# A convolution stage whose scores share TensorE's row strips with the maxima: strips 0 and 1 beside strips 2 and 3

## The reference, cut to what matters

```python
x = x + _L1_conv_ref(_gn(x), ...)

def _L1_conv_ref(x, wq, bq, wk, bk, wv, bv, fc1_w, fc1_b, fc2_w, fc2_b, fuse_w, fuse_b):
    q = conv2d(x, wq, bq, 'SAME').reshape(b, -1, hw)      # 16 channels, 3x3
    k = conv2d(x, wk, bk, 'SAME').reshape(b, -1, hw)      # 16 channels
    v = conv2d(x, wv, bv, 'SAME').reshape(b, c, hw)       # 64 channels
    attn = jnp.einsum('bci,bcj->bij', q, k) * scale
    attn = jax.nn.softmax(attn, axis=-1)
    local = jnp.einsum('bcj,bij->bci', v, attn).reshape(b, c, h, w)
    y = jnp.mean(x, axis=(2, 3))
    y = jax.nn.relu(y @ fc1_w.T + fc1_b)
    y = jax.nn.sigmoid(y @ fc2_w.T + fc2_b)
    glob = x * y[:, :, None, None]
    cat = jnp.concatenate([local, glob], axis=1)
    return conv2d(cat, fuse_w, fuse_b, 'VALID')           # 1x1
```

## Time and profile before

| what | value |
|---|---|
| device time, 3 runs | 11482.52, 11489.68, 11515.75 us; median 11489.68 |
| the profiled execution: its own time, its span | 11510.12 us, 11508.3 us |
| granted TensorE clock, mean of the span | 0.807 of full speed |
| busy in the span | PE 60%, DVE 64%, ACT 42%, POOL 63% |
| convolution stage: first operation of VectorE to its last write of the result | 6044.26 to 6660.72 us |
| products for the maxima (L809), in the stage | 256 MATMUL, 110.7 us busy, 47.9 us of idle TensorE before them |
| products of input and gated term (L867, L869) | 128 and 128 MATMUL |

### The profile page before, as it was taken

The page is one execution under the profiler, slowest core; times in us unless marked ns, Lnnn a source line. Parts: engine busy times, 40 slices in busy tenths (PEclk is TensorE's granted clock), DMA queues, the critical chain, the costliest instruction groups (busy, mean ns, idle before and its releaser), DMA issues. The chain is left out here.

```text
span 11508.3 us, 84579 instructions
## 1 busy us (share of the span) xinstructions
PE 6869.3 (60%) x21895; PEld 2896.9 (25%) x21895; DVE 7327.9 (64%) x5584; ACT 4837.5 (42%) x5351; POOL 7215.9 (63%) x4635
## 2 busy tenths in 40 slices
PE   0178888888888888888878979950000010000569
PEld 0133333333333333333333323320000000000432
DVE  8689999999999999999992257741111111112334
ACT  0066666666666666666652236631111111110123
POOL 0078888888888888888873220017777777775037
PEclk8599999999999999999997679975555555555569
DMA  0145555555555555555551000012222222220022
GB/s 9 31 134 155 152 157 154 156 156 154 156 153 156 153 156 154 157 155 154 156 147 24 1 10 1 1 5 37 18 18 18 18 20 18 18 18 8 3 53 89
DMA packets 388258, 959.55 MB, mean 83 GB/s; under 512 B 124306, under 2 KB 159762, under 8 KB 385762
## 3 DMA queue, kind: packets, MB, share of 16 engines
q1 hardware_dynamic: 303106, 930.59, 29.2%
q0 software_dynamic: 75808, 26.27, 5.2%
q10 hardware_dynamic: 9216, 1.05, 0.1%
HBM read 905.24 MB, written 50.92 MB: 83 GB/s over the span
## 5 line engine op out<-in xcount | busy, mean ns | idle before, releaser
L502 POOL TENSOR_TENSOR hC<-h,Cb 128x1024 f32<-128x1024 f32 x1536 | 3610.4, 2359 | 936.5 <-DVE h L581 935.0
L581 DVE TENSOR_TENSOR_SCAN h<-dA,B_ps 128x1024 f32<-128x1024 f32 x1536 | 3512.4, 2287 | 68.1
L285 PE MATMUL y_ps<-hC,con 128*128 128x512 f32 x6144 | 2909.8, 595 | 92.5 <-DVE gz L587 56.9
L432 ACT ACTIVATE dA<-delta,negA 128x1024 f32<-128x1024 f32 x1536 | 1762.5, 1148 | 1835.6 <-DVE h L581 1835.0
L2514 POOL DMA_INDIRECT g_got<-scratch_node,g_idx x2048 | 1946.1, 950 | 614.4 <-issue 614.2
L573 DVE TENSOR_TENSOR B_ps<-dx,B_ps 128x1024 f32<-128x1024 f32 x1536 | 1856.3, 1208 | 93.2 <-PE B_ps L279 93.2
L2530 PE MATMUL g_ps_y<-g_wout,g_hid 128*128 128x64 f32 x512 | 126.2, 428 | 2248.4 <-ACT g_hid L2570 2248.4
L285 PEld LDWEIGHTS y_ps<-hC,con 128*128 128x128 f32 x6144 | 1136.9, 189 | 1127.3 <-issue 740.5
L279 PE MATMUL B_ps<-Bpart,sel 96*128 96x512 bf16 x3072 | 925.7, 383 | 676.0 <-DVE h L581 674.9
L2600 DVE TENSOR_TENSOR g_e<-g_tgt,g_got 128x128 f32<-128x128 f32 x64 | 27.1, 423 | 1759.9 <-DMA g_got<-scratch_node,g_idx 1759.9
L2554 ACT ACTIVATE g_w_ps<-g_w 128x128 f32<-128x128 f32 x64 | 18.0, 281 | 1941.2 <-DVE g_r L2615 1941.2
(11 more groups left out here) (470 smaller groups left out, 10158.7 us busy)
## 6 DMA issues: line engine op xcount, KB each, us to landing
Cb<-scratch_c_rows SPq DMA_DIRECT2D x3072, 256.0 KB, 3.9
g_got<-scratch_node,g_idx POOLq DMA_INDIRECT x2048
eb_share<-scratch_gate_rows SPq DMA_DIRECT2D x128, 256.0 KB, 3.4
scratch_edge<-g_out SPq DMA_DIRECT2D x64, 384.0 KB
par<-in_ssm SPq DMA_DIRECT2D x48, 395.5 KB, 5.0
scratch_c_rows<-Crow SPq DMA_DIRECT2D x96, 128.0 KB, 3.7
scratch_place<-s_zero SPq DMA_DIRECT2D x4, 1024.0 KB, 10.4
g_tgt<-scratch_place SPq DMA_DIRECT2D x1, 4096.0 KB, 20.8
```

Of the source, the lines that this page charges most:

```text
L285: last = nc.tensor.matmul(y_ps[:, hs], con[:, K_ID:K_ID + P], hC[k % DEEP][:, hs], start=(k == 0), stop=(k == STEPS - 1))
L432: A(dA[k % DEEP][:, :], delta[d][:, :], ACT.Exp, scale=negA[:, n:n + 1]).then_inc(decay_ready, 1)
L502: G.tensor_tensor(hC[k % DEEP][:, :], hst[k % DEEP][:, :], Cb[k % DEEP][:, :], ALU.mult).then_inc(prod_ready, 1)
L581: V.tensor_tensor_scan(hst[k % DEEP][:, ::step], dA[k % DEEP][:, ::step], B_ps[k % 2][:, ::step], 0.0, ALU.mult, ALU.add).then_inc(scanned, 1)
```

## The change

1. The maxima move to row strips 2 and 3 (partitions 64 to 127) and are issued one block to every slot, each half of them straight behind one half of the scores: strips 0, 2, 1, 3. They write other PSUM banks than the scores. A block's products start when `top_read` says that the block before was reduced; the image's first block also waits for `doubled`.
2. For that the queries and keys must lie on partitions 64 to 127 as well. VectorE copies them there (`double`): four copies of 64x512 after each of the first two groups of taps of a pair, 32 in all, each four behind a wait for `conv_read`.
3. Input and gated term of a pair are computed for both images at once with block-diagonal weights, as 128x128 products, in two halves ("res0", "res1", at u = 9 and 11 of the pair before), and go with the bias straight to `t_sb`. The image's fused output is added to `t_sb` later. The per-image event "res" in slot 3 is gone, and so is its place at the stage's end.
4. `search.first_level` is issued by VectorE after the first pair's preparation instead of ahead of it.

The diff, without constants, names and the packing of the weights:

```diff
@@ -655,23 +655,23 @@
 
     def maxima_at(g):
 
-        img, s = g // PER + 1, g % PER
-        return [(img, 2 * (s - 2) + k) for k in range(2)] if 2 <= s <= 5 and 0 <= img < B else []
+        img, i = divmod(g + PER + 2, PER)
+        return (img, i) if 0 <= img < B else None
 
     def events_at(g):
 
         out = []
         img, s = g // PER, g % PER
-        if s in (1, 2, 3) and 0 <= img - 1 < B:
-            out.append((("den", "out", "res")[s - 1], img - 1))
+        if s in (1, 2) and 0 <= img - 1 < B:
+            out.append((("den", "out")[s - 1], img - 1))
         if s == 6 and 0 <= img + 1 < B:
             out.append(("rows", img + 1))
         q, u = at_pair(g, 2)
         if q is not None and u in (8, 12, 13, 14):
             out.append(({8: "gm", 12: "gv", 13: "fc1", 14: "fc2"}[u], q))
         q, u = at_pair(g, 1)
-        if q is not None and u in (7, 15):
-            out.append((f"vt{u // 8}", q))
+        if q is not None and u in (7, 9, 11, 15):
+            out.append(({7: "vt0", 9: "res0", 11: "res1", 15: "vt1"}[u], q))
         return out
 
     def taps_at(g):
...
@@ -699,11 +699,11 @@
         cw = sb("cw", [P, CW_COLS])
         con = sb("con_c", [P, K_COLS])
         xc, sq = sb("cxc", [P, L]), sb("csq", [P, L])
-        xg = [sb(f"cxg{k}", [P, L]) for k in range(3)]
+        xg = [sb(f"cxg{k}", [P, L]) for k in range(2)]
         xpad = sb("xpad", [P, PW, PW])
         st = sb("st", [P, 16])
         S1, GM, S2, GV, YS, HID, Y, BQ = (st[:, i:i + 1] for i in range(8))
-        key, query = ([sb(f"c_{n}{k}", [2 * 32, L]) for k in range(4)] for n in ("key", "query"))
+        key, query = ([sb(f"c_{n}{k}", [P, L]) for k in range(4)] for n in ("key", "query"))
         v_sb = sb("v_sb", [P, L])
         vT = [sb(f"vT{k}", [P, PER, 2, C]) for k in range(2)]
         mrow = sb("mrow", [P, PER])
...
@@ -775,17 +775,29 @@
                 def dve(name, q):
                     pe.wait_ge(dve_done, dve_s.after(name, q))
 
-                def scores(g):
+                def scores(g, half):
 
                     img, j = divmod(g, PER)
-                    if j == 0:
+                    if j == 0 and half == 0:
                         pe.wait_ge(rows_in, img * 32 + 32)
-                    for half in range(2):
-                        if g:
-                            pe.wait_ge(exped, 2 * (g - 1) + half + 1)
-                        rows = strip(half)
-                        M(part_ps[half][:, :], key[img % 4][rows, j * P:(j + 1) * P], query[img % 4][rows, halves[half]],
-                          start=True, stop=True).then_inc(scored, 1)
+                    if g:
+                        pe.wait_ge(exped, 2 * (g - 1) + half + 1)
+                    rows = strip(half)
+                    M(part_ps[half][:, :], key[img % 4][rows, j * P:(j + 1) * P], query[img % 4][rows, halves[half]],
+                      start=True, stop=True).then_inc(scored, 1)
+
+                def maxima(img, i, half):
+                    n = maxima_no[img, i]
+                    if half == 0:
+                        if i == 0:
+                            pe.wait_ge(doubled, 2 * (img // 2) + 2)
+                        if n:
+                            pe.wait_ge(top_read, n)
+                    rows = strip(2 + half)
+                    last = M(top_ps[:, halves[half]], query[img % 4][rows, i * P:(i + 1) * P], key[img % 4][rows, halves[half]],
+                             start=True, stop=True)
+                    if half:
+                        last.then_inc(topped, 1)
 
                 def sums(g):
                     img, j = divmod(g, PER)
@@ -798,17 +810,6 @@
                         last = M(sum_ps[half * C:(half + 1) * C, :], vT[img // 2 % 2][:, j, img % 2, :], E[g % 4][:, halves[half]],
                                  start=j == 0, stop=j == PER - 1)
                     last.then_inc(summed, 1)
-
-                def maxima(img, i):
-                    n = maxima_no[img, i]
-                    if i == 0:
-                        pe.wait_ge(conv_read, 4 * (img // 2) + 2)
-                    if n:
-                        pe.wait_ge(top_read, n)
-                    for half in range(2):
-                        last = M(top_ps[:, halves[half]], query[img % 4][strip(half), i * P:(i + 1) * P],
-                                 key[img % 4][strip(half), halves[half]], start=True, stop=True)
-                    last.then_inc(topped, 1)
 
                 def taps(q, group, tap):
 
...
@@ -860,26 +861,25 @@
                             last = M(side_ps[:, k * P:(k + 1) * P], oT[at % 2][:, k * P:(k + 1) * P], cw[:, CW_FL:CW_FL + P],
                                      start=True, stop=True)
                     else:
-                        q, b = divmod(at, 2)
-                        dve("xg", q)
-                        rows = slice(b * C, (b + 1) * C)
-                        for i in BLK:
-                            M(side_ps[:, i * C:(i + 1) * C], x_sb[rows, q, i * P:(i + 1) * P], con[rows, K_ID + b * C:K_ID + (b + 1) * C],
-                              start=True, stop=False)
-                            last = M(side_ps[:, i * C:(i + 1) * C], xg[q % 3][rows, i * P:(i + 1) * P], cw[rows, CW_FG:CW_FG + C],
+                        dve("xg", at)
+                        for k in range(4):
+                            i = 4 * int(kind[-1]) + k
+                            M(side_ps[:, k * P:(k + 1) * P], x_sb[:, at, i * P:(i + 1) * P], con[:, K_ID:K_ID + P], start=True, stop=False)
+                            last = M(side_ps[:, k * P:(k + 1) * P], xg[at % 2][:, i * P:(i + 1) * P], cw[:, CW_FG:CW_FG + P],
                                      start=False, stop=True)
                     last.then_inc(side_made, 1)
 
                 pe.wait_ge(loaded, 32)
                 for g in slots:
-                    if 0 <= g < ALL:
-                        scores(g)
+                    for half in range(2):
+                        if 0 <= g < ALL:
+                            scores(g, half)
+                        if maxima_at(g):
+                            maxima(*maxima_at(g), half)
                     if 0 <= g - 1 < ALL:
                         sums(g - 1)
                     for event in events_at(g):
                         side(*event)
-                    for block_ in maxima_at(g):
-                        maxima(*block_)
                     for tap in taps_at(g):
                         taps(*tap)
 
@@ -989,6 +989,14 @@
                     if i == 0 and img:
                         dve.wait_ge(side_made, event_no["rows", img - 1] + 1)
                     V.reduce_max(mrow[:, i:i + 1], top_ps[:, :], AX).then_inc(top_read, 1)
+
+                def double(q, group):
+
+                    dve.wait_ge(conv_read, 4 * q + group + 1)
+                    for b in range(2):
+                        for t in (query, key):
+                            last = V.tensor_copy(t[(2 * q + b) % 4][C:P, halves[group]], t[(2 * q + b) % 4][0:C, halves[group]])
+                    last.then_inc(doubled, 1)
 
                 def side(kind, at):
 
@@ -1022,23 +1030,30 @@
                                         side_ps[:, :].rearrange("p (k h c) -> p h k c", k=4, h=2),
                                         rden[:, :].rearrange("p (h k) -> p h k", h=2).unsqueeze(3).broadcast_to([P, 2, 4, C]),
                                         ALU.mult).then_inc(side_read, 1)
+                        dve.wait_ge(side_read, event_no[kind, at] + 1)
+                        here = t_sb[:, at * PER:(at + 1) * PER, :]
+                        V.tensor_tensor(here, here, tmp[:, :, :], ALU.add).then_inc(fin, 1)
+                        dve.wait_ge(fin, at + 1)
                     else:
-                        V.tensor_tensor(tmp[:, :, :], tmp[:, :, :], side_ps[:, :].rearrange("p (i c) -> p i c", i=PER),
-                                        ALU.add).then_inc(side_read, 1)
-                        dve.wait_ge(side_read, event_no[kind, at] + 1)
-                        V.tensor_tensor(t_sb[:, at * PER:(at + 1) * PER, :], tmp[:, :, :],
-                                        cw[:, CR_FB:CR_FB + C].unsqueeze(1).broadcast_to([P, PER, C]), ALU.add).then_inc(fin, 1)
-                        dve.wait_ge(fin, at + 1)
+                        first = 2 * at * PER
+                        here = t_sb[:, first:first + 2 * PER, :].rearrange("p (b i) c -> p i b c", b=2)
+                        bias = cw[:, CR_FB:CR_FB + C].unsqueeze(1).unsqueeze(1).broadcast_to([P, 4, 2, C])
+                        V.tensor_tensor(here[:, 4 * int(kind[-1]):4 * int(kind[-1]) + 4, :, :],
+                                        side_ps[:, :].rearrange("p (i b c) -> p i b c", i=4, b=2), bias, ALU.add).then_inc(side_read, 1)
 
                 dve.wait_ge(loaded, 32)
                 dve.wait_ge(zeroed, 1)
                 V.tensor_scalar(BQ, cw[:, CV_BQ:CV_BQ + 1], SCALE, None, ALU.mult).then_inc(dve_done, 1)
```

(18 more changed lines are left out.)

2 lines of the change are left out of this document (1 added, 1 removed).

## The result

The change takes 11362.6 us (median of 4 runs, 11359.4 to 11374.62) against 11490.43 before (4 runs), a ratio of 0.988 [0.9869, 0.9892]: 128 us faster, where 90 were forecast. The profiled execution has its own time of 11365.2 us, a span of 11363.4 and a mean granted clock of 0.818.

What follows compares the result with a forecast made beforehand. TensorE was taken as the bound, often at 1.2 GHz. Tap halves -55, tap-free halves -13, last slots -11, end -8, start -4.5 sum to -91.5, called 90: 11420 profiled, 11400 median; range 11335 to 11445.

Steps and rivals of the forecast that it cites:

- the rival with the high clock: Four strips hold TensorE at 2.4 GHz in tap-free halves, last slots and start: gain 150 us, 11340; chance 17%.
- signs of being wrong: Tap halves above 70 us or clock below 0.7; fast tap-free halves; first score after 6135; late gathers; other stretches changing.
- Four strips run together: In the stage's slots, two score and two maxima products take one pair plus 0.07 us, 64 times: 4.5 us lost.
- the strips do not overlap: Score and maxima products wait at different times, each slot costs a pair more, some 85 us: 11485; chance 5%.
- The low clock in the tap-free halves and the last slots: TensorE stays mostly at 1.2 GHz there; tap-free halves gain only 13 us, the last 16 slots 11.
- Tap halves: The three halves with taps take 57.6, 62.4 and 62.4 us against 73.7, 82.9 and 80.9: 55 us gained.
- Four buffers of `E` cover: GpSimd's gathers end 12 us later; four buffers cover this until slot 4, else it costs a few us once.
- Copies of 0.4: Each of VectorE's 512-column copies in `double` takes 0.4 us; at 0.69 the gain is 7 us less.
- Start and end: Moving the search brings first scores 4.5 us earlier; one addition replacing "res" and its answers saves 8 us.
- slower: low clock through tap halves: Stalls in slots 2 and 4 keep tap halves at 1.2 GHz: 138 us more, a loss of 48, 11535; chance 3%.

Runs made afterwards that it cites:

- Experiment 1: The changed kernel with the maxima on strips 0 and 1 again, the copies still made but not read: 11466.18 us, ratio 0.9958 to the kernel before.
- part 3 alone: The kernel before with only the block-diagonal input and gated-term products for both images and the later addition of the fused output: 11460.39 us, ratio 0.9954.
- experiment 5: The changed kernel with VectorE reducing a slot's maxima before it answers the slot's event: 11293.39 us, ratio 0.981 to the kernel before.
- experiment 6: The changed kernel with VectorE's copies of queries and keys issued two slots later: 11348.44 us, ratio 0.9856 to the kernel before.
- experiment 3: The changed kernel with input and gated term computed per image by 64-row products in "res", as before: 11403.85 us, ratio 0.991 to the kernel before.
- experiment 7: The changed kernel with VectorE reducing before answering events and copies two slots later, run twice: 11281.98 and 11285.01 us, ratios 0.98 and 0.9802 to before.
- experiment 10: The changed kernel with reduction before answers, copies two slots later, and the search again ahead of the first reduction: 11302.66 us, ratio 0.9818 to before.
- experiment 9: The changed kernel with reduction before answers, copies two slots later, and GpSimd's gathers spread, 16 ahead then two per tap slot: 11278.37 us, ratio 0.9803.
- Experiment 4: The kernel before with only the search moved behind the first pair's preparation on VectorE, 10 runs: 11498.44 us, ratio 0.9989 to the kernel before.

## Why the prediction was right, and where it was off

The direction and the mechanism held, and 11362.6 lies in the range of 11335 to 11445. The size was off by 38 us. The gain of 128 lies outside the 65 to 120 that I called my forecast (57%) and short of the 150 of the rival with the high clock (17%); the range held it because it was drawn out to that rival. Of the signs of being wrong one came: tap-free halves near 43 us with a clock above 0.8, in two of three (44.74 and 38.95 us at 0.89 and 0.87).

- **Four strips run together**: right, but not 64 times. 1.07 us for four products against 1.05 + 0.07 forecast, in 20 slots; in 34 three halves run together behind the wait; ten blocks have no scores beside them. Experiment 1 puts the overlap, with the clock that goes with it, at 90 us of the 128. The rival "the strips do not overlap" would have been about even; with the same strips the kernel is at 11466.
- **The low clock in the tap-free halves and the last slots**: the step that failed. The prediction says "From here I take the low clock, as now", and wrote 56.9, 56.9, 50.6 and 85.8 us. Measured are 49.75, 44.74, 38.95 and 64.65, at clocks of 0.76 to 0.89. Here -24 was forecast and -76 came. The argument was that TensorE would idle more in the new order, two to three us in most of these slots. It idles 5.7, 6.9 and 3.8 us in a whole half, about as much as before (5.7, 5.7 and 5.4 by the two columns of the earlier trace rows), so the argument's premise was wrong. A part of this is on the timeline: the first half of the scores runs inside the wait, so of 2.7 us between the mean's product and the maxima 1.6 are idle (6192.65 to 6195.33). What raised the clock the runs part only roughly. The three tap-free halves have 0.55, 0.60 and 0.61 before; 0.75, 0.67 and 0.71 with part 3 alone; 0.78, 0.72 and 0.75 with all but part 3; 0.76, 0.89 and 0.87 with both; and 0.60, 0.68 and 0.65 with both but the maxima on strips 0 and 1. So the clock is up with either part, and in two of the three halves highest with both. The last case has part 3's products and the old strips, and is lower than part 3 in the old order in two of three, so the order of the products may bear on it too, and experiments 5 and 6 move it with order and waits alone. Which property decides stays open; no run varied one by itself.
- **The rival "the clock stays up"** (11340) named this, with a tap-free half of 43 us. It came half way in the first half, nearly all the way in the other two, and further than the rival in the last 16 slots, where it had about 71. There experiment 3 shows 19 us that hang on "res", of which the forecast knew only a part: it kept 38.6 us for the last eight slots with "their res being gone", where they took 39.6 before with a "res" among them (6607.46 to 6647.04). They took 31.9 in the change, and the eight before them 32.7 for 46.7. (The two terms add up to 85.3, not 85.8.)
- **Tap halves**: 48.3 for 55, a term 7 us too large. (The terms as listed give 57.8 and 62.2 with the four strips' 0.6, for 57.6 and 62.4.) In the second and third it was 63.2 and 61.6 for 62.4, so these were right, but by two errors that cancel: the clock was 0.95 and 0.97, better than taken, and the stall in slot 2's place came out at 3.7 us for 2.6, because the addition into `t_sb` waits for GpSimd. The first took 64.4 for 57.6; the two copies of 2.56 us are 4.3 of that.
- **"Four buffers of `E` cover" the late gathers**: right for `E`, and beside the point. What the lateness costs comes by another way: GpSimd's overdue additions run against the copies. As a cost "those few us once" was the right size (5.0 and 5.5 us, the first tap half of experiment 7 against those of experiments 10 and 9).
- **Copies of 0.4**: right where VectorE has the ports alone (0.41).
- **Start and end**: -8.5 for -4.5, and -6.2 for -8. Experiment 4 has 9.9 us for the earlier first scores in the old order, near the 9.5 forecast; of the 5 that the new order was to give back, 1.3 came (82.4 us to the first scores for 81.1).
- **The rival "slower: low clock through tap halves"**: never in sight, 0.89 to 0.97.

## What to carry to other kernels

When a change takes idle strips of TensorE's array into use, price the stretch at both levels of the clock and ask what in the new order speaks for each; here the forecast was 52 us short (24 for 76) in the stretches that hang on it. When an engine waits in a slot for another's answer, put that answer first in the answering engine's own order: one moved loop gave 80 us, nearly as much as the strips. Before giving VectorE a copy or an addition from SBUF to SBUF, look at what GpSimd does at that time.

## What the runs showed of the hardware

- VectorE's copies of 64 x 512 from SBUF to SBUF take 0.41 us alone, and up to 2.57 beside GpSimd's additions of 2.34 to 2.47; a 128 x 512 addition with both sources in SBUF goes from 0.69 to 2.00. Operations that read PSUM stayed as they were (0.69 and 1.22), and so did copies beside GpSimd's gathers.
- Four fp32 products over 32 rows each, on four strips, take 1.07 us from their start to the next start, two take 1.05, both at the upper clock.
- The tap-free halves ran at a clock of 0.81 to 1.00 in experiments 5 and 7 with TensorE busy for 27 to 33 of 28 to 36 us, and at 0.60 to 0.68 in experiment 1 with TensorE busy for 55 to 63 of 57 to 68.
- Two executions of one kernel can differ in a stretch's clock: the last 16 slots of experiment 7 had 0.76 in one (56.87 us) and 0.92 in the other (50.76 us).
